# Table building and running sums in the spectral stage: the first tiles brought forward, a chained sum, and one product tile from GpSimd to VectorE

## What is computed

```python
xn = layernorm(x)
q, kv = xn @ W_q.T, xn @ W_kv.T            # 4 sequences of 512 rows, 16 heads of 16
qf, kvf = fft(q), fft(kv)                   # over each head's 16 values
qf, kvf = qf / norm(qf), kvf / norm(kvf)    # per row and head
kvf = cumsum(kvf, axis=rows of the sequence)
s = ifft(qf * kvf).real @ W_o.T             # the "spectral" result

logits = xn @ router_w.T                    # 64 experts, the best 8 of each row
buf = the first 64 rows that chose each expert, in row order
y = w_down( silu(gate(buf)) * up(buf) )     # per expert
g = silu(sum of a row's 8 expert results by their shares)
x = x + s * g
```

## Time and profile before

| | us |
|---|---|
| median of 3 runs | 1127.05 |
| lowest and highest | 1126.38, 1132.29 |
| the profiled execution, its own time | 1129.77 |
| its span in the trace | 1128.0 |

### The profile page before, as it was taken

The page is one execution under the profiler, slowest core; times in us unless marked ns, Lnnn a source line. Parts: engine busy times, 40 slices in busy tenths (PEclk is TensorE's granted clock), DMA queues, the critical chain, the costliest instruction groups (busy, mean ns, idle before and its releaser), DMA issues.

```text
span 1128.0 us, 22277 instructions
## 1 busy us (share of the span) xinstructions
PE 990.6 (88%) x6773; PEld 654.5 (58%) x6773; DVE 855.4 (76%) x2247; ACT 668.2 (59%) x1738; POOL 541.2 (48%) x532
## 2 busy tenths in 40 slices
PE   3966889845889999999999999999987899999975
PEld 2645534323455666676676666766654578885543
DVE  4788458846698779768768899999846877775677
ACT  1732435414667865967866666666635877775332
POOL 0478557412664466543444444544411345553774
PEclk9988989966999999999999999999989999999997
DMA  9988699877564456131111001210039445553443
GB/s 340 338 271 305 160 261 311 287 251 227 89 145 102 114 108 151 31 83 38 62 53 39 19 21 38 90 39 1 1 100 320 122 130 143 147 137 97 133 127 99
DMA packets 97023, 155.99 MB, mean 138 GB/s; under 512 B 12272, under 2 KB 67312, under 8 KB 94096
## 3 DMA queue, kind: packets, MB, share of 16 engines
q1 hardware_dynamic: 77184, 115.42, 31.4%
q0 software_dynamic: 19728, 39.21, 16.1%
HBM read 104.84 MB, written 45.02 MB: 133 GB/s over the span
## 4 chain that ended last, share of the span: by engine, by line
PE 55%; DVE 15%; ACT 9%; issue 6%; DMA 4%; DVEq 4%; POOL 3%; POOLq 3%; ACTq 1%; SPq 1%
PE ps L1087 9%; PE ps L1256 6%; PE ps L1150 5%; PE ps L1100 5%; PE ps L1138 5%; PE ps L1118 3%; PE ps L1202 3%; PE ps L1219 3%; ACT arena L1508 2%; PE ps L1274 2%; PE ps L984 2%; POOLq L192 2%; DVE x_sb L1891 2%; PE ps L1001 1%; PE ps L1246 1%
## 5 line engine op out<-in xcount | busy, mean ns | idle before, releaser
L2331 POOL TENSOR_TENSOR arena<-arena 128x512 f32<-128x512 f32 x128 | 175.0, 1429 | 112.9 <-ACT arena L1485 112.9
L1087 PE MATMUL ps<-arena 128*128 128x512 f16 x768 | 177.6, 381 | 1.3 <-ACT arena L1485 1.3
L2336 POOL TENSOR_TENSOR arena<-arena 128x512 f32<-128x512 f32 x64 | 66.6, 1041 | 176.9 <-DVE arena L1985 176.9
L2373 POOL DMA_INDIRECT wvo<-xn_d,idx x79 | 75.5, 956 | 117.1 <-PE ps L1246 97.3
L1087 PEld LDWEIGHTS ps<-arena 128*128 128x128 f16 x768 | 75.1, 98 | 93.4 <-ACT arena L1485 3.5
L1508 ACT ACTIVATE arena<-arena 128x128 f32<-128x128 f32 x256 | 99.2, 390 | 41.2 <-DVEq L1980 41.2
L1484 ACT ACTIVATE arena<-ps 64x512 f32<-64x512 f32 x128 | 76.1, 594 | 52.4 <-DVE arena L1953 48.7
L1150 PE MATMUL ps<-wvo,arena 128*128 128x256 f16 x768 | 96.6, 278 | 5.8 <-DVE arena L1997 3.2
L1100 PE MATMUL ps<-wvo,arena 128*128 128x512 f16 x384 | 94.4, 382 | 5.8 <-ACT arena L1494 2.7
L1953 DVE TENSOR_TENSOR arena<-ps,wvo 128x512 f32<-128x512 f32 x128 | 84.7, 683 | 18.7 <-PE ps L1087 18.6
L1138 PE MATMUL ps<-arena 128*128 128x192 f32 (+1 forms) x512 | 94.8, 329 | 2.4 <-DVE arena L1991 2.4
(11 more groups left out here) (295 smaller groups left out, 2199.4 us busy)
## 6 DMA issues: line engine op xcount, KB each, us to landing
arena<-wqk_d SPq DMA_DIRECT2D x16, 1024.0 KB, 5.8
arena<-in_wgu SPq DMA_DIRECT2D x32, 384.0 KB, 9.7
y_d<-wvo SPq DMA_DIRECT2D x79, 128.0 KB, 2.4
z_d<-wvo SPq DMA_DIRECT2D x8, 1024.0 KB, 4.3
z_d<-wvo SPq DMA_DIRECT2D x2, 4096.0 KB, 25.4
arena<-in_wdn SPq DMA_DIRECT2D x32, 192.0 KB, 12.9
arena<-z_d SPq DMA_DIRECT2D x12, 512.0 KB, 4.3
arena<-z_d POOLq DMA_DIRECT2D x12, 512.0 KB, 6.8
```

Source lines behind the costliest of these rows:

```text
L1087: last = pe.matmul(ps[s][:, :], wqk[gg][:, s * DC + c, w, hh * DH:(hh + 1) * DH], hx[bb][:, :, x, c * P:(c + 1) * P], start=(c == 0 and w ...
L2331: nc.gpsimd.tensor_tensor(qk_s[:, s], qk_s[:, s], sin, ALU.mult).then_inc(sin_done, 1)
```

## The change

- In stage 1 ACT takes the square roots of the first two tiles' sums as soon as they are there, and those of the other 14 tiles at the end. DVE takes the reciprocals of the first two tiles and makes the mask `mk0` before its last sum of squares, POOL runs `normalise(0)` and `normalise(1)`, and PE `running_sum(0, 0)`, all ahead of their `stage_end`. `running_sum(0, 1)` is issued between the two mask steps.
- A running sum is now `tri` times the tile plus the last row of the neighbour's sum `cs[(t - 1) % 2]`, spread by a broadcast column of the identity. It waits for ACT's copy of that sum, and takes two products for every tile but the first of a sequence.
- `LATE` goes from 10 to 9, so tile 9's products move from POOL to DVE.
- POOL does `normalise(t + 2)` after `products(t)` and not before it.
- On ACT `sum_out(0, 0)` comes ahead of the mask copies.
- On DVE the reciprocals of the other 14 tiles follow the stage's beginning, and the two subtractions with `exp_in` are put behind the first `largest`.

```diff
-        LATE = 10
+        LATE = 9
...
+                if tt:
+                    upto(pe, cum_rd, t - 1)
+                    pe.matmul(out, ident[:, P - 1:P].to_broadcast([P, P]), cs[:, (t - 1) % 2], start=True, stop=False)
-                for j in range(tt):
-                    pe.matmul(out, ones[:, :], row(qkv[:, bass.ds(TPB * b + j, 1), D:2 * D]), start=(j == 0), stop=False)
                 pe.matmul(out, tri[:, :], row(qkv[:, bass.ds(t, 1), D:2 * D]), start=(tt == 0), stop=True).then_inc(cum_ps, 1)
+            pipelined(front, back_, pe)
+            running_sum(0, 0)
+            stage_end(pe, 1)
...
             last.then_inc(table0_mm, 1)
+            running_sum(0, 1)
             pe.wait_ge(masks_rd, 2)
...
-            running_sum(0, 0)
-            running_sum(0, 1)
             for t in range(TABLES_AT):
                 spectral(t)
...
+                if t == NT - 2:
+                    done(act, ss_ready, 1)
+                    nc.scalar.activation(flat(ss[:, 0:2]), flat(ss[:, 0:2]), ACT.Sqrt).then_inc(nrm_sq, 1)
...
-            nc.scalar.activation(flat(ss), flat(ss), ACT.Sqrt).then_inc(nrm_sq, 1)
+            nc.scalar.activation(flat(ss[:, 2:NT]), flat(ss[:, 2:NT]), ACT.Sqrt).then_inc(nrm_sq, 1)
...
+            sum_out(0, 0)
             act.wait_ge(table0_mm, 1)
             for n in range(2):
                 nc.scalar.activation(masks[:, n * 512:(n + 1) * 512], ps[6 + n][:, :], ACT.Copy).then_inc(masks_rd, 1)
-            sum_out(0, 0)
             sum_out(1, 1)
             spectral(0)
             act.wait_ge(exp_in, 1)
...
+                if t == NT - 1:
+                    dve.wait_ge(nrm_sq, 1)
+                    nc.vector.reciprocal(flat(ss[:, 0:2]), flat(ss[:, 0:2])).then_inc(norm_ready, 1)
+                    dve.drain()
+                    nc.vector.tensor_scalar(mk0.rearrange("p n h e -> p h n e"), gone.rearrange("p (h n) e -> p h n e", h=2), GONE, None, ALU.is_equal)
+                    dve.drain().then_inc(chosen0, 1)
                 back_(t)
-            dve.wait_ge(nrm_sq, 1)
-            nc.vector.reciprocal(flat(ss[:, 0:2]), flat(ss[:, 0:2])).then_inc(norm_ready, 1)
             dve.wait_ge(w1_in, 32)
             stage_end(dve, 1)
-            nc.vector.tensor_scalar(mk0.rearrange("p n h e -> p h n e"), gone.rearrange("p (h n) e -> p h n e", h=2), GONE, None, ALU.is_equal)
-            dve.drain().then_inc(chosen0, 1)
+            dve.wait_ge(nrm_sq, 2)
             nc.vector.reciprocal(flat(ss[:, 2:NT]), flat(ss[:, 2:NT])).then_inc(norm_ready, 1)
-            nc.vector.tensor_tensor(exA0, lgA0, mxA0[:, :, 0:1].to_broadcast([P, NT, E0]), ALU.subtract)
-            nc.vector.tensor_tensor(ex8, mxA0, mxA0[:, :, 0:1].to_broadcast([P, NT, K0]), ALU.subtract)
-            dve.drain().then_inc(exp_in, 1)
...
             largest(early_keys, keys[:, 0], keys[:, 1])
             dve.sem_inc(chosen0, 1)
+            nc.vector.tensor_tensor(exA0, lgA0, mxA0[:, :, 0:1].to_broadcast([P, NT, E0]), ALU.subtract)
+            nc.vector.tensor_tensor(ex8, mxA0, mxA0[:, :, 0:1].to_broadcast([P, NT, K0]), ALU.subtract)
+            dve.drain().then_inc(exp_in, 1)
             dve.wait_ge(table0_mm, 3)
...
-            stage_end(pool, 1)
             normalise(0)
             normalise(1)
+            stage_end(pool, 1)
             for t in range(NT):
-                if t + 2 < NT:
-                    normalise(t + 2)
                 if t < LATE:
                     upto(pool, cum_rd, t)
                     upto(pool, yT_ps, t - 2)
                     products(pool, nc.gpsimd, t, 0).then_inc(y_ready, 1)
+                if t + 2 < NT:
+                    normalise(t + 2)
```

More of the change, by code:

```diff
@@ L903, in back_ @@
                 last.then_inc(qkv_ps, 1)
-            pipelined(front, back_, pe)
-            stage_end(pe, 1)
             def running_sum(b, tt):
```

## The result

The changed kernel takes 1144.18 us (median of 4 runs, 1142.04 to 1147.48), against 1128.27 for the kernel before, run beside it (median of 4). The ratio is 1.0136 with a 95% interval of 1.0115 to 1.0157: slower by 15 us, where 11.4 were forecast. In the profiled execution (1144.86 us, span 1143.1) stage 3 starts at 144.29 and not at 130.00: 14.3 us of the loss lie in the spectral stage and ahead of it. From there to the end it takes 998.8 us, before it took 998.0. Of the 14.3 some 0.6 are not the change's: DVE's sum of squares of tile 14, ahead of its first changed step, starts at 61.58 in this execution; it starts at 60.92 in the kernel before and at 61.02 in e1, which has the same code up to there.

What follows compares the result with a forecast made beforehand. No engine was full; hand-overs between engines bound the spectral stage, with two nearly equal ends. Terms 13.6 - 1.8 + 0 - 0.4 = +11.4 us on a median of 1127.05 gave 1138.5 us, range 1133 to 1145.

Steps and rivals of the forecast that it cites:

- The rival of the half clock: PE runs at half clock after ACT's stop, with late L950 and slower tail passes: +5 us, 1143.5; chance 0.12.
- ACT goes on: ACT, waiting for late `exp_in`, resumes with tile 1 at 94.8 instead of 81.20: +13.6 us.
- from there to L951: From ACT's resuming to PE's L950 (now L951): 11.5 us where it took 13.3, so -1.8.
- from the indices to stage 3: Remaining product tiles on DVE and PE, now seven: 19.0 us where six took 19.45, so -0.4.
- The opening: Start of the spectral stage: opens about 64.95, 1.1 us later, yet keys start about 69.0 instead of 69.98.
- The table load: ACT's 1.28 us load for the exponentials, expected in idle time ahead of the `exp_in` wait, adding nothing.
- the rival with the load behind the wait: ACT's table load comes after `exp_in`: +1.3 us, or 2.7 with a drain, 1140 to 1141; chance 0.10.
- The restart: After ACT resumes, `products(3)` starts 0.8 us later and PE reaches L950 after 11.5 (bounds 10.9 to 12.7).
- The tail: After tile 9, PE's passes take 2.0 us each; tile 15's products end 11.6 later, the stage 2.9 after that.
- Tile 9 on DVE: Tile 9's products on DVE, beside POOL's six normalisations, end with them and take 4.2 us.
- The chained sums: Running sums built from the neighbour's sum: five `ones` products fewer on PE, about 2.2 us gained in the tail.
- The rival on the other side: DVE's search hides ACT's stop, so the stage ends about 4 us earlier: 1123; chance 0.05.

Runs made afterwards that it cites:

- e1: Changed kernel with the two subtractions and `exp_in` put back ahead of the first search; 1128.01 us, ratio 1.0005.
- e2: Changed kernel with ACT's wait for `exp_in` and its exponentials moved from after spectral(0) to after spectral(4); 1131.47 us, ratio 1.0023.
- e3: Kernel before the change with only the two subtractions and `exp_in` put behind the first search; 1139.46 us, ratio 1.0107.
- e4: Changed kernel with the two subtractions and `exp_in` after four of the first search's eight rounds; 1135.36 us, ratio 1.0059.
- e5: Changed kernel with filler products of ones on PE, six ahead of spectral(8) and ten ahead of spectral(9); 1144.24 us, ratio 1.0127.
- e7: e1 with 16 filler products of ones on PE ahead of spectral(9); 1128.94 us, ratio 0.9992.
- e8: e1 with the running sums made as before, from ones times every earlier tile; 1133.19 us, ratio 1.0034.

## Why the prediction was right, point by point

The mechanism is the one forecast: `exp_in` late stops ACT, ACT stops POOL's tile 3 and PE's tile 4, and PE's L951 stops DVE. e1 and e2 take it away from its two ends, e3 makes it alone, e4 halves it. The size is less good than the mechanism: 1144.18 lies 5.7 us above the 1138.5 forecast and 0.8 inside the top of the range. Of the 5.7, 2.9 are the stage, 0.8 the later stages of the profile, and 2.0 the step from the profiled execution to the median: I took it to stand 2.7 above the median, as before, and it stood 0.7 above. The rival of the half clock had named 1143.5, 0.7 us off, but for the most part by other terms: its late L950 did not come, and of its 5 us the runs show some 2. The terms:

| term | forecast | measured |
|---|---|---|
| ACT goes on (95.44 less 81.20) | +13.6 | +14.2 |
| from there to L951 (10.98 less 13.32) | -1.8 | -2.3 |
| from L951 to the indices (15.75 less 15.92) | 0 | -0.2 |
| from the indices to stage 3 (22.12 less 19.56) | -0.4 | +2.6 |
| sum | +11.4 | +14.3 |

- **The opening** was 0.9 too good. I had the mask at its old 0.69 us; beside POOL's normalisation, which now started first, it took 1.59. That made DVE and ACT set the opening, and not POOL: my 64.4 for them becomes 65.3, where e1 opens (65.36, DVE's first instruction). The 0.6 by which this execution was late from the start make it 65.85, and the keys came at 69.86, not 69.0; without them ACT's restart would be at about the 13.6 forecast. The cheaper subtractions (1.22 and 0.28, not 1.8 together) gave 0.3 of it back.
- **The table load** lay ahead of the wait, as read from the earlier trace rows: loads at 74.97 here and at 90.01 in e2, each with its exponential later. Nothing was added for it, and the rival with the load behind the wait falls.
- **The restart** was right in kind. PE was at half clock from 95.87 (L932, 2.08) and at full clock from 99 on, so L951 came at the early end of its bounds.
- **The tail is the term that was mis-sized**, by 3.0 us. Of these, some 1.3 are from the indices to the end of tile 9 (5.8 us, forecast 4.5) and 1.8 from there to stage 3 (16.3, forecast 14.5). In the second part "a pass with one `ones` product took 2.0 us" was carried to passes that ran at half clock: that of tile 9 took 3.9. With the clock kept at 1.00 (e5) this part took 14.2 us, so the rest of it was right. I had the half clock as a rival and gave it 0.12, holding against it that PE would be no less busy than before; its waits for tiles 8 and 9, 2.02 and 2.68 us, were not in that argument. Its price was too low as well: 1.74 for four products was read where the granted clock was 0.62, and at 0.50 they take 1.91. The filler took 2.1 us out of this stretch (e5) and 2.8 out of the stage without the stop (e7).
- **Tile 9 on DVE.** I let the normalisations hold it for 4.2 us; it took 5.5, as DVE came to it 1.3 us after they had begun and not 2.4, and it ended 0.4 after them. The slowest DVE operations on 128x128 took 1.14 there, as in the earlier trace rows. The rule of the Trainium skill (SBUF — State Buffer, "Who interferes with whom") was borne out, for the mask as well: of two operations that shut each other out, the one that starts first has its way and the other waits. The change had let POOL start first (62.79, the mask 62.80; before, the mask 63.88, POOL 63.89).
- **The chained sums** gave what was forecast (e8: 2.4 against 2.2). The near match is in part chance: I priced five products at full clock, and two of them ran at half. And the broadcast column costs PE no more than a plain product: two such matmuls take 0.60 in e7's tail as two of ones do in e8's.
- **The rival on the other side**, a stop that the search hides, asked for DVE to set the end whatever ACT does. DVE's wait of 12.82 us for L951 is against it. But what it said of the rest, 4 us of gain without the stop, was too much: e1 shows 0.3, and 3.1 with the filler in front of tile 9 (e7), so the clock takes most of what is missing.

What stays open is 1 us between the loss in the stage (14.3) and that of the whole (15.3 by the ratio, 13.0 to 17.7); the profile's later stages hold 0.8 of it, within their scatter.

## What to carry to other kernels

When a signal is moved later on its producer, look up where its consumer waits in program order and list everything queued behind that wait; the signal's own deadline (here the narrow search's end) may be far away while the queue behind the wait is needed at once. Move the wait with the signal, or neither. And where a step is handed to an engine that must share with a neighbour, price it by what runs beside it at that moment, and if the engine that waits is PE, price its first work behind the wait at the low clock too.

## What the runs showed of the hardware

- A VectorE mask (128x1024, f32 to bf16) took 0.69 us before and 1.59 when a GpSimd multiplication had started first; in the first case it was the GpSimd one that was longer (two in 2.62, against 1.04 to 1.06 for one alone). In the second case the two took 2.52: the first was done by 63.9, when PE takes up its result, and by the lengths the mask ran ahead of the second.
- In e1 PE's granted clock was 1.00 when a wait of 4.01 us began (108.9) and 0.53 over the 6.5 us behind it. In the changed kernel it fell to 0.50 behind waits of 2.02 and 0.75 us with 0.44 of work between them, and stayed there through the wait of 2.68. With ten or sixteen dense filler products in the last gap (e5, which also has six in the one ahead, and e7) it was 1.00 behind it. So PE's waits are paid twice here, once as waiting and once in the next pass.
- On two chips the kernel before took 1166.0 and 1170.0 us, 3.3% to 3.7% longer than on the others. In the four traces from there engines, ACT above all, stand idle for up to 9.2 us at places where the profile names a releaser outside the core, which none of the ten traces taken where the kernel before took 1127 to 1129 us show. The cause was not tried.
